# Dense attention with rings of eight and a new order, idle sums in the down product, and the maxima of eight heads in one pass

## The reference

```python
x = x + _L0_xattn_ref(_layernorm(x), ctx, ctx, mask)       # 16 heads of 16
x = x + _L0_ffn_ref(_layernorm(x), w_gate, w_up, w_down)   # 256 -> 768 -> 256, fake-quantised
x = x + _L1_xattn_ref(_layernorm(x), ctx, ctx, Wq, bq, ..., ln_gamma, ln_beta)  # 16 heads of 64
x = x + _L1_ffn_ref(_layernorm(x), W1, b1, W2, b2, Wr, br) # 8 experts, argmax routing
...
q = (query @ Wq + bq); k = (key @ Wk + bk); v = (value @ Wv + bv)
attn = softmax(q k / 8); out = attn v @ Wo + bo + query
return layernorm(out) * ln_gamma + ln_beta
...
for i in range(num_experts):                # every expert is added for every token,
    xi = x * mask_i                         # with xi = 0 where the token isn't routed to it
    out = out + (relu(xi @ W1[i] + b1[i]) @ W2[i] + b2[i])
```

## Time and profile before

| what | value |
| --- | --- |
| median of 3 runs | 1651.63 us (1647.52 to 1653.64) |
| the profiled execution's own time | 1649.6 us |
| its span, first to last instruction | 1647.8 us |
| TensorE busy | 1389.3 us (84%) |
| VectorE, ScalarE, POOL busy | 1183.1, 1047.2, 431.9 us |
| mean granted TensorE clock | 0.920 |

### The profile page before, as it was taken

The page is one execution under the profiler, slowest core; times in us unless marked ns, Lnnn a source line. Parts: engine busy times, 40 slices in busy tenths (PEclk is TensorE's granted clock), DMA queues, the critical chain, the costliest instruction groups (busy, mean ns, idle before and its releaser), DMA issues. The chain is left out here.

```text
span 1647.8 us, 35334 instructions
## 1 busy us (share of the span) xinstructions
PE 1389.3 (84%) x11229; PEld 1184.0 (72%) x11229; DVE 1183.1 (72%) x2102; ACT 1047.2 (64%) x2716; POOL 431.9 (26%) x735
## 2 busy tenths in 40 slices
PE   5788888898867689998788888898888867999997
PEld 3455555686744468898677778787777757999996
DVE  6688777887645569086477777777777766888885
ACT  4677778574466656463566666666666625888885
POOL 5444443000000001002123222323232313444443
PEclk9999999899988889999799989989998878999998
DMA  7311010472366778743413232232323135511110
GB/s 225 100 31 35 29 35 28 144 280 90 113 195 199 231 240 268 261 139 109 169 65 114 93 103 77 83 121 76 102 76 120 38 129 210 195 45 54 54 47 9
DMA packets 106773, 194.91 MB, mean 118 GB/s; under 512 B 13474, under 2 KB 72893, under 8 KB 100288
## 3 DMA queue, kind: packets, MB, share of 16 engines
q1 hardware_dynamic: 96320, 160.13, 29.0%
q0 software_dynamic: 10176, 33.57, 6.8%
q10 hardware_dynamic: 192, 0.13, 0.0%
HBM read 128.49 MB, written 68.03 MB: 119 GB/s over the span
## 5 line engine op out<-in xcount | busy, mean ns | idle before, releaser
L1996 ACT ACTIVATE c_w_raw<-c_ps_score,c_shift 128x128 f32<-128x128 f32 x512 | 184.0, 393 | 172.3 <-DVE c_shift L1872 135.9
L2373 PE MATMUL d_ps_hT<-d_zT,d_w_tile 128*128 128x128 f32 x1248 | 148.5, 278 | 1.6 <-DVE d_zT L2480 1.6
L2373 PEld LDWEIGHTS d_ps_hT<-d_zT,d_w_tile 128*128 128x128 f32 x1248 | 145.3, 195 | 2.3 <-DVE d_zT L2480 2.3
L2386 PE MATMUL d_ps_y<-d_w_parts,d_hT 128*128 128x256 f32 x936 | 121.8, 287 | 1.8 <-DVE d_res L2511 1.8
L1996 ACT ACTIVATION_READ_ACCUMULATOR c_w_raw<-c_ps_score,c_shift 128x1 f32 x512 | 118.8, 232 | 0.0
L2386 PEld LDWEIGHTS d_ps_y<-d_w_parts,d_hT 128*128 128x128 f32 x936 | 114.6, 191 | 2.0 <-DVE d_res L2511 2.0
L581 ACT ACTIVATE a_probT<-a_ps_probT 128x512 f32<-128x512 f32 x128 | 71.1, 623 | 66.2 <-PE a_ps_probT L368 66.2
L459 DVE TENSOR_REDUCE a_row_max<-a_ps_score 128x8 f32<-128x1024 f32 x64 | 78.0, 1218 | 48.6 <-PE a_ps_score L357 48.6
L2546 ACT ACTIVATE d_h<-d_ps_hT,d_b1T 128x128 f32<-128x128 f32 x312 | 88.7, 367 | 37.8 <-PE d_ps_hT L2373 37.8
L2499 DVE TENSOR_TENSOR d_w_parts<-d_w,d_w_parts 128x1024 fp32r<-128x1024 f32 x78 | 95.2, 1221 | 23.7 <-ACT d_w_parts L2558 23.7
L1754 PE MATMUL c_ps_proj<-c_xnT,c_wq 128*128 128x256 f32 x768 | 105.9, 288 | 0.0
(11 more groups left out here) (299 smaller groups left out, 3731.3 us busy)
## 6 DMA issues: line engine op xcount, KB each, us to landing
keys_scratch<-b_out SPq DMA_DIRECT2D x64, 256.0 KB, 3.6
values_scratch<-b_out SPq DMA_DIRECT2D x64, 256.0 KB, 3.6
c_kT<-keys_scratch SPq DMA_DIRECT2D x16, 1024.0 KB, 6.4
d_w<-w_in SPq DMA_DIRECT2D x16, 1024.0 KB, 8.0
split_scratch<-b_split SPq DMA_DIRECT2D x12, 1024.0 KB, 4.7
c_v_more<-values_scratch SPq DMA_DIRECT2D x24, 512.0 KB, 3.9
b_ctx_high<-split_scratch POOLq DMA_DIRECT2D x16, 512.0 KB, 6.1
b_ctx_low<-split_scratch POOLq DMA_DIRECT2D x16, 512.0 KB, 7.5
```

The lines of the kernel that those rows point to most:

```text
L1996: last = act.activation(prob[:, n, j, :], ps_score[:, n % 2, j, :], ACT.Exp, scale=float(KD) ** -0.5, bias=shift[:, n, j:j + 1], accum_out ...
L2373: last = pe.matmul(ps_hT[:, f, :], w1_tile[:, half, k, n * P:(n + 1) * P], zT[:, s, k, :], start=(k == 0), stop=(k == ND - 1))
L2386: last = pe.matmul(ps_y[:, 0:D], hT[:, s, a, f, :], w2_parts[:, half, b, n, :], start=(f == 0 and (a, b) == PARTS[0]), stop=(f == FB - 1 a ...
```

## The change

In the feed-forward part the idle sums leave the key blocks. They follow every second tile of the down product, with three `w2` buffers; ScalarE's copy of the sums and their store come at the end of that stage, ahead of the last store of x2. PE's and SP's loops over the tiles are written out.

In the dense attention x2 is loaded once, into a ring of eight (`x2`), and `xn` is a ring of eight too: it serves the queries and the residual. The bias of the output is added on TensorE, by one matmul per block of two rows (bias, high and low half) with ones. Queries and bq are scaled by 1/8, so the exponentials need no scale, and the maximum of eight heads is taken negated in one pass and is their bias at once; `shift` is gone. `normalise_output` is two passes with two operations each instead of three. POOL keeps one pass (x plus beta). The order of the step changes on TensorE and VectorE (below) and on ScalarE, where the copy of the turned x now stands ahead of the first exponentials, the copies of the last probT of the block before between the first two sets of exponentials, and the copy of zT and the query copies behind the second set, and the hardware loop covers eight blocks. The product of bv and Wo moves to step 0, and from 128 to 2 rows. In the experts ScalarE's pass for `at_tile` goes ahead of its copies to `other`.

The diff, cut to what is spoken of:

```diff
-        w2 = x_space[:, 0:4 * D].rearrange("p (e d) -> p e d", d=D)
-        idle = x_space[:, 0:BANK].rearrange("p (g d) -> p g d", g=2)
-        down_int = x_space[:, BANK:BANK + NF * D // 4].bitcast(I16)
+        w2 = [raw_at(f"w2_{n}", [P, 4, D], offset)
+              for n, offset in enumerate((address["yT"] + 4 * (2 * T - ITEM), address["upT"], address["gateT"]))]
+        idle = out2[:].rearrange("p (g d) -> p g d", g=2)
...
                 def load_w2(i):
                     g, f = divmod(i, FB)
-                    if i >= 1:
-                        sp.wait_ge(idle_part, i)
+                    if i >= 3:
+                        sp.wait_ge(idle_part, i - 2)
                     for e in range(4):
-                        sp.dma_start(w2[:, e, :], w2_dram[4 * g + e][:, f, :]).then_inc(w2_loaded, 16)
+                        sp.dma_start(w2[i % 3][:, e, :], w2_dram[4 * g + e][:, f, :]).then_inc(w2_loaded[i % 3], 16)
...
-                sp.wait_ge(product_done, 2 * NC * NF)
-                load_w2(0)
-                w2_pieces = 1
                 for n in range(ALL):
                     store_block(n)
-                    if n % IDLE_EVERY == IDLE_EVERY - 1 and w2_pieces < 2 * FB:
-                        load_w2(w2_pieces)
-                        w2_pieces += 1
-                    if n == KEYS:
-                        sp.wait_ge(idle_ready, 1)
-                        for e in range(4):
-                            sp.dma_start(idle_dram[e:NE:4].unsqueeze(0), idle[32 * e:32 * e + 1]).then_inc(idle_stored, 16)
                 sp.wait_ge(block_done, ALL)
                 sp.dma_start(wq_raw[:], wq_dram).then_inc(wq_loaded, 16)
-                sp.wait_ge(idle_stored, 64)
                 for n in range(NO):
                     sp.wait_ge(block_stored[n], 16 * ((ALL + NO - 1 - n) // NO))
-                for t in range(4):
-                    step(t, t)
-                with sp.Fori(1, NB // 4) as i:
-                    for s in range(4):
-                        step(4 * i + s, s)
-                for t in range(NB - 3, NB):
-                    store(t, t % 4)
+                for t in range(NB):
+                    step(t, t % 4)
+                store(NB - 3, (NB - 3) % 4)
+                store(NB - 2, (NB - 2) % 4)
+                sp.wait_ge(idle_ready, 1)
+                for e in range(4):
+                    sp.dma_start(idle_dram[e:NE:4].unsqueeze(0), idle[32 * e:32 * e + 1]).then_inc(idle_stored, 16)
+                store(NB - 1, (NB - 1) % 4)
                 sp.wait_ge(wq_loaded, 16)
+                sp.wait_ge(idle_stored, 64)
...
+                        if n == 1:
+                            pe.wait_ge(relu_b1_ready, 1)
+                        if n % 2 == 1:
+                            idle_sums(n // 2)
+
+                for c in range(NC):
+                    down(c, c % 2)
...
-                pool.wait_ge(bo_added, 1)
-
-                def residuals(t, u, i):
...
+                def residual(t, w):
+                    pool.wait_ge(xn_ready, t + 1)
+                    pool.tensor_tensor(x2[:, w, :], x2[:, w, :], beta[:], ALU.add).then_inc(x2_beta_ready, 1)
...
                 def output(b, u):
                     t, s = b - 1, (u + 1) % 2
-                    if inside(b, FIRST, NB - 5):
+                    if inside(b, 4, NB):
+                        bank_after_logits(b)
+                    else:
                         pe.wait_ge(xnT_ready, b + 5)
-                    else:
-                        bank_after_logits(b)
-                    pe.wait_ge(attnT_ready, 2 * t + 2)
                     if isinstance(b, int) and b == 1:
                         pe.wait_ge(w_split, 2)
+                        pe.wait_ge(bo_ready, 1)
+                        pe.wait_ge(ones_ready, 1)
+                    pe.matmul(ps_aux[:, 0:D], two_ones[:], bo_parts[:], start=True, stop=False)
+                    pe.wait_ge(attnT_ready, 2 * t + 2)
                     for n, (blk, (a, c)) in enumerate(product(range(BLKS), PARTS)):
                         last = pe.matmul(ps_aux[:, 0:D], attnT[:, s, a, blk, :], wo[:, c, blk, :],
-                                         start=(n == 0), stop=(n == BLKS * len(PARTS) - 1))
+                                         start=False, stop=(n == BLKS * len(PARTS) - 1))
...
                 def maxima(b, n):
-                    m = NU * b + n + 1
                     dve.wait_ge(scores_done, 2 * b + n // 2 + 1)
-                    dve.tensor_reduce(row_max[:, n, :], ps_score[:, n % 2], AX_X, ALU.max).then_inc(max_done, 1)
-                    dve.wait_ge(max_done, m)
-
-                    dve.tensor_scalar(shift[:, n, :], row_max[:, n, :], -float(KD) ** -0.5, None, ALU.mult)\
-                       .then_inc(shift_ready, 1)
+                    dve.tensor_reduce(neg_max[:, n:n + 2, :], ps_score[:], AX_X, ALU.max, negate=True).then_inc(max_done, 1)
...
-                def normalise_output(t, u, i):
+                def normalise_output(t, u, w, i):
 
                     s = u % 2
+                    dve.wait_ge(mv_o_done, t + 1)
+                    dve.scalar_tensor_tensor(proj[:, s, :], proj[:, s, :], mv_o[:, s, 0:1], gamma[:],
+                                             ALU.subtract, ALU.mult).then_inc(scaled_done, 1)
                     dve.wait_ge(rstd_o_done, t + 1)
-                    dve.tensor_scalar(proj[:, s, :], proj[:, s, :], mv_o[:, s, 0:1], rstd_o[:, s, :],
-                                      ALU.subtract, ALU.mult).then_inc(normed_done, 1)
-                    dve.wait_ge(normed_done, t + 1)
-                    dve.tensor_tensor(proj[:, s, :], proj[:, s, :], gamma[:], ALU.mult).then_inc(scaled_done, 1)
                     dve.wait_ge(scaled_done, t + 1)
                     dve.wait_ge(x2_beta_ready, t + 1)
                     if inside(t, 4, NB - 1):
                         dve.wait_ge(zx_stored[u], 16 * (uses(t, i) - 1))
-                    dve.tensor_tensor(x3[:, u, :], proj[:, s, :], x2_late[:, u, :], ALU.add).then_inc(x3_ready, 1)
+                    dve.scalar_tensor_tensor(x3[:, u, :], proj[:, s, :], rstd_o[:, s, :], x2[:, w, :],
+                                             ALU.mult, ALU.add).then_inc(x3_ready, 1)
...
                 def exponentials(b, n):
                     m = NU * b + n + 1
-                    act.wait_ge(shift_ready, m)
+                    if n % 2 == 0:
+                        act.wait_ge(max_done, 2 * b + n // 2 + 1)
                     if inside(b, 1, NB):
                         act.wait_ge(probT_done, m - NU)
                     for j in range(HB):
-                        last = act.activation(prob[:, n, j, :], ps_score[:, n % 2, j, :], ACT.Exp, scale=float(KD) ** -0.5,
-                                              bias=shift[:, n, j:j + 1], accum_out=row_sum[:, n, j:j + 1])
+                        last = act.activation(prob[:, n, j, :], ps_score[:, n % 2, j, :], ACT.Exp,
+                                              bias=neg_max[:, n, j:j + 1], accum_out=row_sum[:, n, j:j + 1])
```

309 lines of the change are left out of this document (154 added, 155 removed).

## The result

The changed kernel took 1543.7 us (median of 4 runs, 1543.2 to 1546.22), the kernel before 1649.72 us in the same comparison: a ratio of 0.9358, 95% interval 0.9335 to 0.9381. The forecast was 1549. The profiled execution spans 1541.5 us, 106.3 less than the one before.

The account below looks back on a forecast made before the run. Bounds: weight waits of idle sums in the blocks, TensorE in down, two TensorE gaps and lower clock in attention. Terms -70 + 9 + 2.5 - 3 - 40 - 1 = -102.5 from 1649.6 give 1547, as median 1549 us; range 1525 to 1588.

Parts of the forecast that it names:

- Blocks: Key and value blocks without the idle sums: product ends near 631 instead of 701.5, -70 us (bounds -46 and -75).
- the walk through ScalarE's units: Key blocks: twelve ScalarE units of 6.14 us from 452 end at 525.7, so quantised silu starts near 529.5.
- the term for the turn to the values, transposes and clock: Key and value blocks: 1.5 us wait at the turn from keys to values, 3 us for transposes and clock.
- the 4 us in which TensorE was to stand for ScalarE's first quantisations: Blocks: with some 62 blocks done, TensorE waits about 4 us for ScalarE's two first quantisations; 66 blocks follow.
- Sets in down: Down product: 16 sets of idle sums at 0.57 us each, all on the path, +9 us.
- End of down and start of the attention: Last set, copy and four stores ahead of the last x2 store, +2.5 us; bias product moved to step 0, -3 us.
- Loop: Dense attention: block of 15.1 instead of 16.4 us over 31 steps, -40 us (bounds -62 and nothing).
- The ring: Dense attention: chain through VectorE's statistics, maxima, exponentials, probT copies and TensorE that sets the block, 15.1 us.
- both passes lie on the ring: Dense attention: both eight-head maxima passes delay exponentials, 1.22 us instead of 0.68 plus the shift's 0.17.
- The third rival: Dense attention: eight-head pass gives back the loop's gain, loop stays near 16 us, 1577 us; chance 0.06.
- The clock rival: Attention loop: clock keeps falling behind the remaining 1.4 us gap; 1599 us in each block, 1574 in half; chance 0.15.
- The rival of waits for w2: Down product: each of 16 sets waits 8.6 us for w2, 138 us, 1687 us; chance 0.02.

Follow-up runs that it names:

- the ten profiles: Profiles of the ten kernels with the new feed-forward part, whose down product starts between 636.6 and 641.4 us.
- the experiment with early logits: Changed kernel with the two logits matmuls directly behind the turn of z, ahead of the weighted values: 1652.44 us, ratio 1.0013.
- a version that closed a gap on TensorE and left `route` ahead of the divisions: Kernel before, with the second half's weighted values ahead of the logits and the turn of x: 1686.8 us, ratio 1.0215.

## Why the prediction was right, and where not

- *Blocks:* forecast -70, measured -65.8. Quantised silu was to start near 529.5 and starts at 529.9, so the walk through ScalarE's units was right. Down was to start near 633 and starts at 638.1 (636.6 to 641.4 over the ten profiles); the second half of the stage took 108 us where I had 103.5. Most of the missing 5 us is in the term for the turn to the values, transposes and clock (4.5 us), which was mis-sized. Of the 4.76 us of the earlier trace rows I left 1.5, and the wait is 3.99 us now. Behind it the matmuls are slow (1.22 and 1.05 us for two, later 0.62), at a granted clock of 0.50 from 541 to 547 us. The rest is spread. Down's first matmul waits 3.3 us for its input behind the last block, where I had about 2. And the 4 us in which TensorE was to stand for ScalarE's first quantisations are 0.3 us, but only some 58 blocks were done by then, not 62; these two nearly cancel.

```profile
541.45 1.22 PE L1046 MATMUL b_ps<-b_w_parts,b_ctx_high 128*128 128x512 f32 x2 [3.99 <-DMA b_ctx_low<-split_scratch]
...
629.82 0.62 PE L1046 MATMUL b_ps<-b_w_parts,b_ctx_high 128*128 128x512 f32 x2
```

- *Sets in down:* forecast +9, measured +11.4 over the stage, which holds 15 of the sets: 0.76 us per set. I took the distance from a set's start to the next product in the key blocks, 0.57 us, as its price; in down TensorE also loses about 0.1 us ahead of a set and 0.1 us at the first matmul behind it. The term was taken as all on the path, and it is.
- *End of down and start of the attention:* forecast +2.5 and -3, together -0.5, measured -2.0. Which of the two was off wasn't tried.
- *Loop:* forecast -40 with 15.1 us per block, measured -48.3 with 14.8. The gap was forecast at 1.4 us, ended by the copy of probT, and is 1.24 to 1.30; the clock was to be over 0.97 and is 0.98. The ring is the one that I walked, and the rows follow it: weighted values to the end of the second scores 4.1 us (955.93 to 960.04; I had 4.3), maxima 1.27 with what stands ahead, exponentials and copies of probT from 961.42 to the last exponential at 965.29, VectorE's divisions and statistics to 966.78 (1.5 us, I had 1.62), maxima 1.23, exponentials from 968.12 to 969.51, copies 1.09, weighted values at 970.73. Together 14.8 us. The 0.3 us per block, 9 us in 31, are small terms taken too long. What the walk did not see is the second path, 0.2 us shorter: TensorE without a pause from 955.93 to the end of the next scores at 966.53.
- *Price of the eight-head pass:* "both passes lie on the ring" holds for the changed kernel, but it does not give two equal prices, as the expectation of up to 33 us had it. The second path caps what the second half can give at 0.2 us per block, and the first half gives 0.5. Together that is 17 us by the times and 18.2 from the first to the last maxima. The third rival did not come: the loop is not near 16 us. What the prediction says in passing, that the one-pass maxima cost, is right.
- *The clock rival* did not come, and the experiment with early logits shows how near it is: two matmuls in another place bring the lower clock back and cost 109 us, the longer wait included. The rival of waits for w2 was priced at 8.6 us per set; even with one load at a time it is 0.9 in 6 of them.
- *Sum:* -65.8 + 11.4 - 2.0 - 48.3 - 1.6 against -70 + 9 - 0.5 - 40 - 1. The errors are +4, +2, -1.5, -8 and -0.6 us. They partly cancel, and that the whole comes out at -106 for -102.5 is luck to that extent. Of the 5 us between 1549 and 1543.7 another 2 are the median of before, 1651.63 when I forecast and 1649.72 beside the changed kernel.

## What to carry to other kernels

Fewer, larger passes on an engine that is not the bound are no gain by themselves: when the next engine can start on half of the result, the pass in two halves gives it the first half sooner, here 17 us of 1544. Ask of each half of a block apart what else has to be done before its result is used: the half from which TensorE waited gave 0.5 us per block, the half that TensorE's other work covered only 0.2, until that work became the longer path. And before an instruction is moved on one engine, list what is queued behind its reader on the others: a version that closed a gap on TensorE and left `route` ahead of the divisions lost 37 us.

## What the runs showed of the hardware

A gap of 1.3 us in each block of 14.8 us on TensorE left the clock at its higher level; one of 2.9 us in the same place took it to the lower one behind each gap (weighted values 1.98 instead of 1.09 us), and a single one of 2.75 us elsewhere did so too (granted clock 0.50). In the kernel before, 1.94 us in two gaps with 0.6 us of work between had done so as well. And VectorE passes with two SBUF inputs beside POOL passes of 0.74 us stretched from 0.475 to 0.69 us and from 0.484 to 0.77 us, while a VectorE pass with one of its inputs in PSUM did not.
